# Projecting the last key tiles of two batches together in a cross-attention kernel

## The chip, the cores and the metric

The kernel runs on one core of a Trainium2 chip. Its time is the device time of one execution in microseconds (us), as the median of several runs.

## What is computed

One layer on x (32 batches, 64 tokens, 128 features): cross-attention onto a context of 1601 keys per batch, masked by length, then a windowed self-attention, then a quantized feed-forward part, each added to x. Only the cross-attention is touched:

```
q: layernorm(x) @ Wq, k: ctx @ Wk, v: ctx @ Wv, 16 heads of 64
qh = rms_norm(qh, q_norm_w); kh = rms_norm(kh, k_norm_w)
scores = einsum('bhld,bhsd->bhls', qh, kh) * (1.0 / np.sqrt(HEAD_DIM))
scores = where(s < x_seqlens[b], scores, NEG_INF)
attn = softmax(scores, axis=-1)
x = x + (attn @ vh, heads joined) @ Wo
```

## The kernel before

The context of a batch is cut into NC = 13 key tiles: twelve of P = 128 keys and a last one of LAST = 65. The key weights are folded into the queries beforehand, so the scores come from the raw context. The projection of the keys is still needed for one thing: each key's sum of squares per head, from which the reciprocal of its norm (rrms) is made. A tile of keys, c of batch p (n = p * 13 + c), goes through these steps:

- SyncE loads it in four DMAs into a stage buffer (`load_stage`), in blocks of 32; the last tile has a buffer of its own and a fifth DMA for its last key.
- VectorE turns it (`turn`), ScalarE rounds it to `cT_hi` (`split_hi`), GpSimd forms the rest `cT_lo` (`split_lo`).
- TensorE projects it (`project`): three matmuls into each of two banks, `k_ps0` and `k_ps1`, 512 columns each. ScalarE squares the banks (`square`), VectorE sums them per head into `ssq` (`sum_squares`).
- Ten steps later TensorE computes the scores (`score`, six matmuls into `s_ps0` and `s_ps1`). VectorE masks and scales them into the arena (`scale`) and keeps the maximum over the tiles (`keep_best`).
- Twenty steps after a tile's scores GpSimd subtracts the maximum (`shift`), ScalarE takes the exponential, TensorE multiplies by the context rows (`values`, sixteen matmuls into `u_ps`).

Every engine walks through the same steps (p, c), written by `each_step`, in its own fixed order. In a step (p, c) TensorE does: projection of tile n + 10 (KEYS_AHEAD), scores of tile n, values of tile n - 20. VectorE does: maximum of tile n - 1, scaling of tile n (two halves, with the turn of tile n + 12 between them), sum of squares of tile n + 10. So the last tile of batch p is projected in step 2 of batch p itself. Further work of VectorE per batch: in step 1 it turns the block of maxima (`turn_blocks`, L847), in steps 2 and 3 it reduces it (`best_of_blocks`, L854), in step 2 it forms the mean squares of the late tiles (L809) and in step 3 their norms (`newton`, L69 to L73). GpSimd's shift in a step waits for that step's `keep_best`.

Batches 2 to 30 are a hardware loop of one batch per pass; batches 0, 1, 31 and two draining rounds are written out. Before them come 20 query steps (projection, norm and turning of the queries), into which the first key tiles are woven; `query(i)` is step i. There no values run up to step 7 of batch 1; in these first steps GpSimd folds the squares in half before VectorE sums them (`fold_squares`, L502).

Semaphores are counted by `Turns`: `x.ended(n)` is the count when unit n has been done. The rows of the context that `values` needs are loaded once per batch in step 9 of SyncE.

## Time and profile before

| | |
|---|---|
| median of 3 runs | 2409.81 us (2409.37 to 2410.38) |
| the profiled execution, and its span | 2404.72 us, 2402.9 us |
| TensorE busy | 2310.5 us, 96% |
| VectorE busy | 2094.6 us, 87% |
| GpSimd busy | 1491.6 us, 62% |
| ScalarE busy | 1368.2 us, 57% |
| mean granted TensorE clock | 0.991 |
| query stage, up to the first scores | about 128 us |
| batches 0 and 1 | 128.7 to 231.2 us |
| one batch in the loop | about 59.6 us |

PE is TensorE (PEld its weight loads), DVE VectorE, ACT ScalarE, POOL GpSimd, SP SyncE. A busy time says how long an engine had work in hand; a row of a time line gives the start, the duration and, in square brackets, how long the engine had been idle before and what ended that. Neighbouring matmuls overlap, so start to start is the time one costs.

### The profile page before, as it was taken

The numbers are of one execution on the slowest core, as the hardware profiler recorded it, in microseconds if no ns is written. First come the engines' busy times: TensorE is split into PE (matmuls) and PEld (weight loads), VectorE is DVE, ScalarE is ACT, GpSimd is POOL, SyncE is SP. The second block draws the span as 40 slices with busy tenths as digits, with TensorE's granted clock in tenths as the row PEclk, the third lists the DMA queues.
The fourth block names the chain that finished last, engine by engine and source line by source line (L and its number), as shares of the span: only waits on it lengthen the run. The fifth ranks groups of instructions, "written<-read, shape, count | busy, mean of one in ns | idle before, by whom it ended". The sixth has DMA issues, their size and how long they took to land. (4 is left out here: it accounts for less than half of the span.)

```text
span 2402.9 us, 57401 instructions
## 1 busy us (share of the span) xinstructions
PE 2310.5 (96%) x16343; PEld 1955.8 (81%) x16343; DVE 2094.6 (87%) x3382; ACT 1368.2 (57%) x2594; POOL 1491.6 (62%) x1069
## 2 busy tenths in 40 slices
PE   7988999999999999999999999999999998899985
PEld 4667888888888888888888888888888888788743
DVE  8789999999999999999999999999999998468776
ACT  6744555555555555555555555555555554455646
POOL 4556777777777777777777777777777773001100
PEclk9999999999999999999999999999999999999987
DMA  3431222222222222222222222222222214421000
GB/s 114 182 85 46 55 54 54 54 54 54 54 54 54 54 54 54 54 55 57 57 54 54 54 54 54 54 54 54 54 54 54 54 38 134 155 90 37 2 1 18
DMA packets 442651, 145.04 MB, mean 60 GB/s; under 512 B 365360, under 2 KB 425680, under 8 KB 442448
## 3 DMA queue, kind: packets, MB, share of 16 engines
q1 hardware_dynamic: 442432, 143.50, 24.0%
q8 instruction: 49, 0.80, 0.1%
q10 hardware_dynamic: 144, 0.52, 0.1%
q14 instruction: 26, 0.21, 0.0%
HBM read 109.17 MB, written 34.73 MB: 60 GB/s over the span
## 5 line engine op out<-in xcount | busy, mean ns | idle before, releaser
L465 POOL TENSOR_TENSOR probs<-arena,best_all 128x1024 f32 (+2 forms) x397 | 943.5, 2377 | 420.0 <-DVE best L842 399.3
L1094 PEld LDWEIGHTS u_ps<-rows,probs 128*128 128x128 f32 x6656 | 803.0, 192 | 56.3 <-issue 15.3
L1094 PE MATMUL u_ps<-rows,probs 128*128 (+1 forms) x6656 | 813.9, 276 | 10.0 <-ACT probs L670 5.0
L827 DVE SCALAR_TENSOR_TENSOR arena<-s_ps,mask,rrms 128x512 f32 (+2 forms) x832 | 604.0, 727 | 117.9 <-PE s_ps L971 116.5
L670 ACT ACTIVATE probs<-probs 128x1024 f32<-128x1024 f32 (+1 forms) x416 | 441.5, 1062 | 411.9 <-POOL probs L465 397.5
L802 DVE TENSOR_REDUCE ssq<-squares 128x16 f32<-128x1024 f32 (+2 forms) x416 | 490.7, 1180 | 38.2 <-ACT squares L628 36.6
L628 ACT ACTIVATE squares<-k_ps 128x512 f32<-128x512 f32 (+1 forms) x832 | 452.2, 592 | 42.5 <-PE k_ps L971 22.2
L842 DVE TENSOR_TENSOR best<-best,arena 128x1024 f32<-128x1024 f32 (+1 forms) x352 | 444.7, 1263 | 0.2
L969 PE MATMUL k_ps<-w_hi,cT_hi 128*128 128x512 f32 (+1 forms) x832 | 361.9, 435 | 5.2 <-ACT squares L628 3.5
L622 ACT ACTIVATE cT_hi<-cT 128x128 fp32r<-128x128 f32 (+1 forms) x416 | 130.1, 313 | 367.6 <-DVE cT L793 367.6
L969 PE MATMUL s_ps<-q_hi,cT_hi 128*128 (+2 forms) x832 | 330.4, 397 | 3.3 <-DVE arena L827 3.0
L971 PE MATMUL k_ps<-w_hi,cT_lo 128*128 128x512 f32 (+1 forms) x832 | 328.6, 395 | 0.0
L970 PE MATMUL k_ps<-w_lo,cT_hi 128*128 128x512 f32 (+1 forms) x832 | 327.2, 393 | 0.0
L970 PE MATMUL s_ps<-q_lo,cT_hi 128*128 (+2 forms) x832 | 327.2, 393 | 0.0
L971 PE MATMUL s_ps<-q_hi,cT_lo 128*128 (+2 forms) x832 | 327.1, 393 | 0.0
L507 POOL TENSOR_TENSOR cT_lo<-cT,cT_hi 128x128 fp32r<-128x128 f32 (+1 forms) x416 | 300.3, 722 | 37.1 <-ACT cT_hi L622 36.7
L969 PEld LDWEIGHTS s_ps<-q_hi,cT_hi 128*128 128x128 f32 (+1 forms) x832 | 153.6, 185 | 46.7 <-DVE arena L827 7.4
L971 PEld LDWEIGHTS s_ps<-q_hi,cT_lo 128*128 128x128 f32 (+1 forms) x832 | 153.1, 184 | 40.0
L970 PEld LDWEIGHTS s_ps<-q_lo,cT_hi 128*128 128x128 f32 (+1 forms) x832 | 153.5, 184 | 39.2
L971 PEld LDWEIGHTS k_ps<-w_hi,cT_lo 128*128 128x128 f32 (+1 forms) x832 | 152.9, 184 | 39.5
L969 PEld LDWEIGHTS k_ps<-w_hi,cT_hi 128*128 128x128 f32 (+1 forms) x832 | 154.5, 186 | 33.4 <-issue 8.9
L970 PEld LDWEIGHTS k_ps<-w_lo,cT_hi 128*128 128x128 f32 (+1 forms) x832 | 154.5, 186 | 19.8
(246 smaller groups left out, 2201.4 us busy)
## 6 DMA issues: line engine op xcount, KB each, us to landing
stage<-in_ctx SPq DMA_DIRECT2D x1536, 16.0 KB, 1.7
rows<-in_ctx SPq DMA_DIRECT2D x32, 768.0 KB
queries<-probs SPq DMA_DIRECT2D x16, 1024.0 KB, 4.0
q_plain<-queries SPq DMA_DIRECT2D x32, 512.0 KB, 3.2
best_all<-best_rows SPq DMA_DIRECT2D x31, 512.0 KB, 3.7
u_transposed<-uT_sb SPq DMA_DIRECT2D x124, 128.0 KB, 2.6
a_uT<-u_transposed SPq DMA_DIRECT2D x10, 1024.0 KB, 4.9
arena<-u_transposed SPq DMA_DIRECT2D x6, 1024.0 KB, 5.0
```

What stands on the lines that cost most here:

```text
L465: pool.tensor_tensor(probs[0:r, slot_of(c, PRING), :], scores_at(b, c), best_all[0:r, bass.ds((b % 2) * HL, HL)], ALU.subtract).then_inc(s ...
L507: pool.tensor_tensor(cT_lo[:, c, 0:r], cT[:, 0:r], cT_hi[:, c, 0:r], ALU.subtract).then_inc(lo_ready.sem, 1)
L622: act.activation(cT_hi[:, c, 0:rows_of(c)], cT[:, 0:rows_of(c)], ACT.Copy).then_inc(hi_ready.sem, 1)
L628: act.activation(squares[0:rows_of(c), half(h)], k_ps[h][0:rows_of(c), :], ACT.Square).then_inc(squared.sem, 1)
L670: act.activation(tile, tile, ACT.Exp).then_inc(probs_ready.sem, 1)
L802: dve.tensor_reduce(ssq[0:r, c * H:(c + 1) * H], squares[0:r, :].rearrange("p (h d) -> p h d", d=HD)[:, :, 0:width], AX_X, ALU.add).then_i ...
L827: dve.scalar_tensor_tensor(out=scores_at(p, c, h * HALF, HALF).rearrange("p (h l) -> p h l", l=L), in0=s_ps[h][0:r, :].rearrange("p (h l) ...
L842: dve.tensor_tensor(best[0:r, :], so_far, scores_at(p, c), ALU.max).then_inc(kept.sem, 1)
L969: pe.matmul(out, cT_hi[:, c, 0:r], hi, start=True, stop=False)
L970: pe.matmul(out, cT_hi[:, c, 0:r], lo, start=False, stop=False)
L971: return pe.matmul(out, cT_lo[:, c, 0:r], hi, start=False, stop=True)
L1094: last = pe.matmul(u_ps[g // 3][:, at:at + UW], probs[0:r, s, g * P:(g + 1) * P], rows, start=(c == 0 and g % 3 == 0), stop=(c == NC - 1), ...
```

## The change

Two batches form a pair. The even batch's last tile is filled up: besides its own 65 keys it takes SHARED = 63 keys of the odd batch's last tile (`load_shared`, eight DMAs). It is turned, split, projected, squared and summed with all 128 rows (`key_rows`). The odd batch's last tile is `borrowed`: it is still loaded, turned and split, since its scores need it, but no longer projected, squared, folded or reduced. Its 65 sums of squares come from elsewhere. 63 rows are carried from the even batch's `ssq` to a corner of `tmp` by a DMA (`load_shared_ssq`, step 7 of the even batch); VectorE copies them into place in step 2 of the odd batch. The two keys left over in each pair, 32 in all, form one extra tile, which is loaded, turned, split, projected, squared and reduced within the query steps 3 to 7; its sums go to memory (`left_ssq`), from where each pair's two rows are fetched.

The loop now runs over pairs 1 to 14, with two batches per pass; batch 30 is written out. The load of the context rows moves from SyncE's step 9 to step 11, and one of its waits goes.

```diff
@@ -170,6 +173,13 @@
 QUERY_STEPS = TILES + CARRY_Q
 KEYS_FROM = 5
 CHUNK = 4
+PAIR_KEYS = 2 * NC - 1
+SHARED = P - LAST
+LEFT = LAST - SHARED
+LEFT_KEYS = B // 2 * LEFT
+LEFT_FROM = 3
+LEFT_IN = 16 * LEFT * D // SIDE
+TAIL_IN = (16 * (3 * D // SIDE + 1), 16 * (D // SIDE + 1))
 
 
 def each_step(eng, query, step, keys_from=KEYS_FROM):
@@ -181,14 +191,37 @@
     for p in (0, 1):
         for c in range(NC):
             step(p, c, On(p, c))
-    with eng.Fori(2, B - 1) as p:
-        for c in range(NC):
-            step(p, c, On())
-    for p in (B - 1, B, B + 1):
+    with eng.Fori(1, B // 2 - 1) as pair:
+        for odd in range(2):
+            for c in range(NC):
+                step(pair * 2 + odd, c, On(pair=pair, odd=odd))
+    for p in (B - 2, B - 1, B, B + 1):
         for c in range(NC):
             step(p, c, On(p, c))
 
 
+def tile_ahead(c, on, ahead):
+
+    later, c = divmod(c + ahead, NC)
+    batch = on.odd + later
+    return on.pair + batch // 2, batch % 2, c
+
+
+def key_number(pair, odd, c):
+
+    return pair * PAIR_KEYS + (odd * NC + c)
+
+
+def borrowed(odd, c):
+
+    return odd == 1 and c == NC - 1
+
+
+def key_rows(odd, c):
+
+    return P if odd == 0 else rows_of(c)
+
+
 def slot_of(c, ring):
 
     return c % ring if c < NC - 1 else ring
@@ -251,6 +284,8 @@
         y0 = sb("y0", [P, NC * H])
         tmp = sb("tmp", [P, NC * H])
         rrms = sb("rrms", [P, NC * H])
+        ssq_shared = tmp[:, EARLY * H:EARLY * H + H]
+        ssq_left = ssq_shared[0:LEFT_KEYS, :]
         qkw = sb("qkw", [P, 3])
         len_i = sb("len_i", [P, B], I32)
         cT = sb("cT", [P, P])
...
+            def load_shared(p, s):
+                first = (NC - 1) * P
+                for g in range(D // SIDE):
+                    dims = slice(g * SIDE, (g + 1) * SIDE)
+                    sp.dma_start(stage[g * SIDE + 1:(g + 1) * SIDE, s, 2 * SIDE:3 * SIDE],
+                                 ctx_in[bass.ds(p + 1, 1), first:first + SIDE - 1, dims].rearrange("b k i -> (b k) i")
+                                 ).then_inc(stage_in[s], 16)
+                    sp.dma_start(stage[g * SIDE:(g + 1) * SIDE, s, 3 * SIDE:4 * SIDE],
+                                 ctx_in[bass.ds(p + 1, 1), first + SIDE - 1:first + 2 * SIDE - 1, dims].rearrange("b k i -> (b k) i")
+                                 ).then_inc(stage_in[s], 16)
+
+            def store_left():
+                sp.wait_ge(left_steps, 6)
+                sp.dma_start(left_out, ssq_left[:, :]).then_inc(shared_in, 16)
+
+            def load_shared_ssq(pair, p):
+                sp.wait_ge(rrms_ready.sem, rrms_ready.ended(p, 6))
+                if isinstance(pair, int) and pair == 0:
+                    sp.wait_ge(shared_in, 16)
+                sp.dma_start(ssq_shared[0:SHARED, :], ssq[LAST:P, (NC - 1) * H:NC * H]).then_inc(shared_in, 16)
+                sp.dma_start(ssq_shared[SHARED:LAST, :], left_out[bass.ds(pair * LEFT, LEFT), :]).then_inc(shared_in, 16)
+
+            def load_stage(p, c, odd):
                 s = slot_of(c, RING)
                 sp.wait_ge(turned.sem, turned.ended(p * NC + c - back(c, RING)))
+                if c == NC - 1 and isinstance(p, int) and p == 0:
+                    sp.wait_ge(left_steps, 1)
+                if c == NC - 1 and odd == 0:
+                    load_shared(p, s)
                 if c == 0 and isinstance(p, int) and p == 0:
                     sp.wait_ge(consts_ready, 4)
                 full = rows_of(c) // SIDE
@@ -406,7 +475,13 @@
 
             def step(p, c, on):
                 if on.load:
-                    load_stage(p + 1, c)
+                    load_stage(p + 1, c, 1 - on.odd)
+                if c == 0 and isinstance(p, int) and p == -1:
+                    load_left()
+                if c == NC - 1 and isinstance(p, int) and p == -1:
+                    store_left()
+                if c == 7 and on.scores and on.odd == 0:
+                    load_shared_ssq(on.pair, p)
                 if c == 5 and on.queries:
                     load_q(p + 1)
                 if c == NC - 1 and on.finish and not ending(p):
...
-                if c == 9 and on.scores:
-                    if not isinstance(p, int) or p > 0:
-                        sp.wait_ge(rows_in, p * 32)
-                    sp.wait_ge(valued.sem, valued.ended(p * NC - NC - 1))
+                if c == 11 and on.scores:
+                    sp.wait_ge(valued.sem, valued.ended(p * NC - NC))
...
+                if i == LEFT_FROM + 1:
+                    act.wait_ge(left_steps, 1)
+                    act.activation(cT_hi[:, NC - 1, 0:LEFT_KEYS], cT[:, 0:LEFT_KEYS], ACT.Copy).then_inc(left_steps, 1)
+                if i == LEFT_FROM + 3:
+                    act.wait_ge(left_steps, 4)
+                    for h in range(2):
+                        last = act.activation(squares[0:LEFT_KEYS, half(h)], k_ps[h][0:LEFT_KEYS, :], ACT.Square)
+                    last.then_inc(left_steps, 1)
 
             def split_q_hi(p):
                 act.wait_ge(q_in, p * 16 + 16)
...
-                if on.keys:
+                if on.keys and not borrowed(*tile_ahead(c, on, KEYS_AHEAD)[1:]):
                     for h in range(2):
-                        square(n + KEYS_AHEAD, at_step(p, c, KEYS_AHEAD)[1], h)
+                        square(n + KEYS_AHEAD, *tile_ahead(c, on, KEYS_AHEAD), h)
                 if on.turn:
-                    split_hi(n + TURN_AHEAD, at_step(p, c, TURN_AHEAD)[1])
+                    split_hi(n + TURN_AHEAD, *tile_ahead(c, on, TURN_AHEAD)[1:])
...
+                if i == LEFT_FROM:
+                    dve.wait_ge(stage_in[RING], LEFT_IN)
+                    dve.transpose(cT[:, 0:LEFT_KEYS], stage[:, RING, 0:LEFT_KEYS]).then_inc(left_steps, 1)
+                if i == LEFT_FROM + 4:
+                    dve.wait_ge(left_steps, 5)
+                    dve.tensor_reduce(ssq_left[:, :], squares[0:LEFT_KEYS, :].rearrange("p (h d) -> p h d", d=HD),
+                                      AX_X, ALU.add).then_inc(left_steps, 1)
...
-            def sum_squares(n, c, folded=False):
-                r = rows_of(c)
+            def sum_squares(n, pair, odd, c, folded=False):
+                r = key_rows(odd, c)
+                if borrowed(odd, c):
+                    dve.wait_ge(shared_in, pair * 32 + 48)
+                    dve.tensor_copy(ssq[0:r, c * H:(c + 1) * H], ssq_shared[0:r, :]).then_inc(summed.sem, 1)
+                    return
                 if folded:
-                    dve.wait_ge(halved, n - KEYS_AHEAD + 1)
+                    dve.wait_ge(halved, key_number(pair, odd, c) - KEYS_AHEAD + 1)
                 else:
-                    dve.wait_ge(squared.sem, squared.ended(n))
+                    dve.wait_ge(squared.sem, squared.ended(key_number(pair, odd, c)))
                 width = HD // 2 if folded else HD
                 dve.tensor_reduce(ssq[0:r, c * H:(c + 1) * H],
...
+                if i == LEFT_FROM + 2:
+                    pe.wait_ge(left_steps, 3)
+                    for h in range(2):
+                        last = product(k_ps[h][0:LEFT_KEYS, :], NC - 1, LEFT_KEYS, w_hi[:, half(h)], w_lo[:, half(h)])
+                    last.then_inc(left_steps, 1)
+
+            def project(n, pair, odd, c):
+                r, k = key_rows(odd, c), key_number(pair, odd, c)
                 pe.wait_ge(lo_ready.sem, lo_ready.ended(n))
+                if isinstance(n, int) and n == 0:
+                    pe.wait_ge(left_steps, 5)
                 for h in range(2):
-                    pe.wait_ge(squared.sem, squared.ended(n - 1, h + 1))
-                    product(k_ps[h][0:rows_of(c), :], c, w_hi[:, half(h)], w_lo[:, half(h)]).then_inc(keys.sem, 1)
+                    pe.wait_ge(squared.sem, squared.ended(k - 1, h + 1))
+                    product(k_ps[h][0:r, :], c, r, w_hi[:, half(h)], w_lo[:, half(h)]).then_inc(keys.sem, 1)
 
             def score(p, n, c):
                 if c == 0:
...
-                if on.keys:
-                    project(n + KEYS_AHEAD, at_step(p, c, KEYS_AHEAD)[1])
+                if on.keys and not borrowed(*tile_ahead(c, on, KEYS_AHEAD)[1:]):
+                    project(n + KEYS_AHEAD, *tile_ahead(c, on, KEYS_AHEAD))
```

TensorE, loop, around the projection of the last tile (k_ps: key banks, s_ps: score banks, u_ps: values). Before:

```order
L1094 MATMUL u_ps2<-rows1,probs 128x129 x2
L1038 REGISTER_ALU
L1040 ISA
L969 MATMUL k_ps0<-w_hi,cT_hi 65x512
L970 MATMUL k_ps0<-w_lo,cT_hi 65x512
L971 MATMUL k_ps0<-w_hi,cT_lo 65x512
L1040 REGISTER_ALU
L969 MATMUL k_ps1<-w_hi,cT_hi 65x512
L970 MATMUL k_ps1<-w_lo,cT_hi 65x512
L971 MATMUL k_ps1<-w_hi,cT_lo 65x512
L1051 ISA
L969 MATMUL s_ps0<-q_hi,cT_hi 128x512
```

After, in the odd batch's half of the loop:

```order
L1211 MATMUL u_ps2<-rows1,probs 128x129 x2
L1168 ISA
L1078 MATMUL s_ps0<-q_hi,cT_hi 128x512
L1079 MATMUL s_ps0<-q_lo,cT_hi 128x512
L1080 MATMUL s_ps0<-q_hi,cT_lo 128x512
```

The values of step 1 are now followed at once by the scores of step 2; the six matmuls between them are gone.

VectorE, loop, step 2 (ssq: sums of squares, best_row: reduced maxima, ms: mean squares). Before:

```order
L827 SCALAR_TENSOR_TENSOR arena<-s_ps,mask,rrms 128x512
L800 ISA
L802 TENSOR_REDUCE ssq<-squares 65x16
L854 TENSOR_REDUCE best_row<-u_sb 128x16
L809 TENSOR_SCALAR ms<-ssq 128x80
L840 ISA
L842 TENSOR_TENSOR best<-best,arena 128x1024
```

After, in the odd batch's half:

```order
L938 SCALAR_TENSOR_TENSOR arena<-s_ps,mask,rrms 128x512
L903 ISA
L904 COPY ssq<-tmp 65x16
L965 TENSOR_REDUCE best_row<-u_sb 128x16
L918 TENSOR_SCALAR ms<-ssq 128x80
L951 ISA
L953 TENSOR_TENSOR best<-best,arena 128x1024
```

A copy stands where the reduction stood; all else keeps its place.

## Rows read from the trace of the kernel before

**Rows 1.** Busy time in stretches: us, busy (x instructions), clock, DMA share, GB/s.

```profile
231.00:1960.00 1729.00, 1728.71 (x10587) 1507.22 (x10586) 1587.35 (x2408) 1003.69 (x1886) 1306.03 (x870) 1.00 0.24 54
```

**Rows 2.** Time line of TensorE, batch 19, steps 2 to 5: start, duration, what.

```profile
1252.00 0.48 PE L969 MATMUL k_ps<-w_hi,cT_hi 128*65 128x512 f32 x1
...
1253.46 0.39 PE L969 MATMUL s_ps<-q_hi,cT_hi 128*128 x1
...
1259.43 1.95 PE L1094 MATMUL u_ps<-rows,probs 128*128 x16
...
1268.67 1.96 PE L1094 MATMUL u_ps<-rows,probs 128*128 x16
```

**Rows 3.** Time line of VectorE, batch 19, steps 1, 2 and 6.

```profile
1251.48 1.20 DVE L802 TENSOR_REDUCE ssq<-squares 128x16 f32<-128x1024 f32 x1
...
1253.94 1.23 DVE L842 TENSOR_TENSOR best<-arena 128x1024 f32 x1
...
1256.59 1.20 DVE L802 TENSOR_REDUCE ssq<-squares 65x16 f32<-65x1024 f32 x1
...
1272.90 0.75 DVE L827 SCALAR_TENSOR_TENSOR arena<-s_ps,mask,rrms 128x512 f32 x1 [0.48 <-PE s_ps L971]
```

**Rows 4.** Time line of GpSimd, batch 19, step 2.

```profile
1255.42 2.38 POOL L465 TENSOR_TENSOR probs<-arena,best_all 128x1024 f32 x1 [3.52 <-DVE best L842]
```

**Rows 5.** Time line of ScalarE, batch 19, steps 3 and 5.

```profile
1257.83 1.07 ACT L670 ACTIVATE probs<-probs 128x1024 f32<-128x1024 f32 x1 [1.35 <-POOL probs L465]
1258.80 1.06 ACT L628 ACTIVATE squares<-k_ps 128x512 f32<-128x512 f32 x2
...
1267.38 1.06 ACT L670 ACTIVATE probs<-probs 128x1024 f32<-128x1024 f32 x1 [1.37 <-POOL probs L465]
```

**Rows 6.** Time lines of VectorE and GpSimd in the query stage.

```profile
26.17 1.81 DVE L743 TENSOR_SCALAR arena<-arena 128x16 f32<-128x16 f32 x1
...
30.52 0.18 DVE L743 TENSOR_SCALAR arena<-arena 128x16 f32<-128x16 f32 x1
...
26.05 1.90 POOL L484 TENSOR_TENSOR arena<-arena 128x1024 f32<-128x1024 f32 x1
```

**Rows 7.** Time lines of TensorE and ScalarE, batch 31, steps 2 to 4.

```profile
1970.68 1.95 PE L1094 MATMUL u_ps<-rows,probs 128*128 128x129 f32 x16
1972.38 0.48 PE L969 MATMUL s_ps<-q_hi,cT_hi 128*128 128x512 f32 x1
...
1974.33 2.05 PE L1094 MATMUL u_ps<-rows,probs 128*128 128x129 f32 x16 [0.31 <-ACT probs L670]
1976.14 0.48 PE L969 MATMUL s_ps<-q_hi,cT_hi 128*128 128x512 f32 x1
...
1973.22 1.06 ACT L670 ACTIVATE probs<-probs 128x1024 f32<-128x1024 f32 x1 [3.14 <-POOL probs L465]
```

**Rows 8.** Time lines of VectorE and GpSimd, batch 1, step 2.

```profile
181.21 2.30 DVE L842 TENSOR_TENSOR best<-arena 128x1024 f32<-128x1024 f32 x1
...
184.95 0.66 DVE L802 TENSOR_REDUCE ssq<-squares 65x16 f32<-65x512 f32 x1
...
181.15 1.28 POOL L502 TENSOR_TENSOR squares<-squares 65x512 f32<-65x512 f32 x1 [1.49 <-ACT squares L628]
```

**Rows 9.** Time lines of TensorE and ScalarE, query step 6 and its end.

```profile
40.49 0.66 PE L1000 MATMUL u_ps<-ident,arena 128*128 128x128 f32 x4 [0.58 <-ACT probs L582]
...
46.84 0.31 ACT L622 ACTIVATE cT_hi<-cT 128x128 fp32r<-128x128 f32 x1 [0.22 <-DVE cT L793]
```

**Rows 10.** DMA queues, 231 to 291 us, then 400 to 1900: packets, MB, share.

```profile
q8 instruction: 3, 0.05, 0.4%
...
q1 hardware_dynamic: 337891, 80.98, 24.3%
```

**Rows 11.** The loop's branch line at 1240 to 1243 us, and the weight loads behind.

```profile
L184 PEldq COMPARE_BRANCH x1: 208/208/208, 1240.8 to 1240.8; - x1
...
1242.84 0.19 PEld L969 LDWEIGHTS k_ps<-w_hi,cT_hi 128*128 128x128 f32 x1
```

97 lines of the change are left out of this document (61 added, 36 removed).

## Prediction

> **What bounds the kernel now.** I read the busy times of the long middle stretch first, then the time line of one odd batch on every engine, then the places where the pattern breaks (batch 1, batch 31, the query stage).
>
> From 231 to 1960 us runs the loop over batches 2 to 30. TensorE is busy 1728.7 of its 1729 us, VectorE 1587 (92%), GpSimd 1306, ScalarE 1004, and the granted clock is 1.00, the upper level of 2.4 GHz [rows 1]. A step (one key tile) takes about 4.57 us on TensorE: projection 1.46, scores 1.4, values 1.7. So at first sight every matmul taken out shortens the time. But "busy" only says that TensorE's gaps are small, not that the other engines have room. The question is how early each tile's exponentials are ready before TensorE wants them.
>
> Take batch 19, an odd one inside the loop. Step 2 holds the projection that the change removes. It starts at 1252.00 and the scores after it at 1253.46: 1.46 us, with 65 keys in the tile [rows 2]. One step later, in step 3, TensorE starts the values matmuls at 1259.43 [rows 2]. Their exponentials ended at 1257.83 + 1.07 = 1258.90 [rows 5]: only 0.53 us in hand. In step 5 it is worse: values at 1268.67 [rows 2], exponentials ended 1267.38 + 1.06 = 1268.44 [rows 5], 0.23 us in hand. That is no accident of one tile. VectorE carries extra work in steps 1 to 4 (turning the best-score block, two reductions of it, the late key norms) and falls behind: it has no idle time until step 6, where it waits 0.48 us for scores again [rows 3].
>
> How little can be in hand? Batch 31 shows it, since from its step 3 on the kernel projects no keys, and its TensorE step is as short as the changed one. There the exponentials end at 1973.22 + 1.06 = 1974.28 and the values start at 1974.33, marked as waiting for ScalarE [rows 7]: 0.05 us is the least. The step shows a second price: values to next scores takes 1976.14 - 1974.33 = 1.81 us after a wait, against 1972.38 - 1970.68 = 1.70 without one [rows 7]. A wait costs 0.11 us to refill the pipe.
>
> **The odd batches in the loop (14 of them).** Removed are six matmuls of 1.46 us in step 2. The chain that ends in step 3's exponentials doesn't use them: VectorE's best-score maximum at 1253.94, GpSimd's subtraction 1255.42 to 1257.80 [rows 3, 4], ScalarE's exponential to 1258.90 [rows 5]. Nor can that chain start sooner, since VectorE's run-up to it begins with the scores of step 1, ahead of the removed work. So step 3's values move from 1259.43 to 1258.90 + 0.05 = 1258.95: 0.48 us gained, 0.98 lost to the new wait. After the refill 0.37 us is left for what follows.
>
> Then step 5. Its room is 0.23 - 0.05 = 0.18 us, unless VectorE gets faster as well. VectorE loses the reduction at 1256.59, 1.20 us long, and gets a copy of 65x16 in its place [rows 3]. The copy is small, but where it stands counts: it would start at about 1256.59, in the middle of GpSimd's subtraction (until 1257.80). The query stage has just such a pair. VectorE's L743, 128x16, takes 0.18 us with GpSimd's long operation not running, and 1.81 us where that one starts just before it: it ends at 27.98, GpSimd's operation at 26.05 + 1.90 = 27.95 [rows 6]. So I take it that the copy is held until GpSimd is done and ends at 1257.83, against 1257.79 for the reduction. VectorE is not earlier but 0.04 us later. Step 5's values then move by 0.18 - 0.04 = 0.14 us, less another refill of 0.11: 0.03 us per odd batch, **0.4 us for 14**. From step 6 on VectorE waits for TensorE again, and the small gain stays.
>
> The Trainium skill ("SBUF — State Buffer", section "SBUF: two separate sides") states this as a rule: one port pair is shared by VectorE and GpSimd under an exclusive lock, and the loser is blocked for the other's whole instruction; the trace agrees. Without this rule the copy would take some 0.2 us and the next rival would be the forecast.
>
> Even batches: the last tile has 128 keys in place of 65. The matmuls write 512 columns per row either way, and the reduction takes 1.20 us for 128 rows and for 65 [rows 3]. I cost this at nothing; should a row count matter after all, it falls in step 2 of even batches, where nothing is taken out and step 3 still has its 0.53 us in hand.
>
> **Batch 1.** No values run before step 7, so VectorE leads. Its maximum takes 2.30 us instead of 1.2, since GpSimd's folding of the very tile that is now borrowed starts 0.06 us before it [rows 8]. The fold goes (1.1 us), and the reduction of 0.66 becomes a copy of about 0.2, with no GpSimd work to hold it: 0.4. Together **-1.5 us** (bounds 0 and -2.5: the projection, the fold and the reduction gone, against other work that fills in).
>
> **Batch 31.** Its step 3 is bound by the same chain today, and the copy meets GpSimd's subtraction again. **0** (bounds 0 and -1.0).
>
> **The extra tile of 32 keys** runs in the query stage: on TensorE 1.46 us at the end of its step 5, of which the 0.58 us idle in the next step absorbs a part [rows 9]: 0.9. Two squares on ScalarE, 1.06 us [rows 5], where it idles only 0.22 us: 0.8. A transpose and a reduction (0.3 and 1.13) on VectorE and two small splits (0.3 and 0.46): VectorE is partly idle there, and GpSimd waits: 0.8. Together **+2.5 us**; bounds 0 (all of it in gaps) and 4.7 (their plain sum).
>
> **SyncE.** Eight more DMAs for each even batch's last tile, two for the sums of squares, and the load of the rows moved from step 9 to step 11. All are read or used a full three steps (13 us) or more after they are issued, and the last tile's issue is followed by a wait for the transposed result. Cost 0; if the cover failed, it would show as VectorE waiting for a stage DMA.
>
> **Sum.** -0.4 - 1.5 + 0 + 2.5 = +0.6 us: 2404.7 us of the profiled execution becomes 2405.3. The median of the runs is 5.1 us above that execution (2409.8), so I forecast **2410.4 us**. A difference under 0.2% (4.8 us) can't be told from no change.
>
> **Rival 1: the copy isn't held.** [Rows 6] show a one-input arithmetic operation, not a copy. If it runs through, VectorE is up to 1.0 us earlier from step 3 on, step 5 isn't tight any more, and the 0.37 us of step 3 survives: 14 x 0.37 = 5.2, batch 31 gains 1.0, and with -1.5 + 2.5 the sum is -5.2 us: 2404.6. For it: the operation differs. Against it: same engine, same kind of operands, same width. Chance 0.18.
>
> **Rival 2: TensorE's saving counts in full**, as its 99.98% busy share suggests: 16 x 1.46 = 23.4, less 2.5: 2388.9 us. It needs step 3's exponentials 1 us earlier than today; nothing ahead of them changes. Chance 0.05.
>
> **Rival 3, slower: the loop's code no longer stays on the engines.** The loop's body now holds two batches. In its first pass, 231 to 291 us, TensorE's instruction queue brought in three packets [rows 10], each 0.4% x 16 x 60 / 3 = 1.3 us long; from 400 to 1900 us only the data queue moved anything [rows 10]. So the old body stays resident; a doubled one may not, and then each of 13 jumps back waits for code. TensorE's branch is at 1240.8 and the first weights of the next pass load at 1242.84 [rows 11]: 2.0 us of waiting are hidden. A delay of one packet costs nothing; two packets and a DMA's way of 1.4 us (the shortest landing in the profile's list of DMAs) would be 4.0 us by estimate, 2.0 of them seen: 13 x 2.0 = 26 us, 2436. It decides from a delay of 2.4 us a pass. Chance 0.10.
>
> The Trainium skill ("Runtime: NRT & Kernel Launch", section "Instruction fetch mechanics") says that a taken branch whose target isn't in the current two-page window forces a DMA fetch, which speaks against a doubled body; the trace of the old loop differs, since it brought three pages in and none again. By the rule alone the old loop would have fetched as well, and the change would halve the number of fetches.
>
> **How the numbers follow.** Forecast 0.62 (2408 to 2412, mostly by the extra tile), rival 1 0.18, rival 2 0.05, rival 3 0.10, and 0.05 for the extra tile at its full price with batch 1 giving nothing. The range 2402 to 2415 takes in the forecast, rival 1 and the bounds of the extra tile. Faster by over 0.2%, 0.21: rival 2, half of rival 1 (it lies on the limit), some of the forecast's lower end. Slower, 0.15: rival 3 and the extra tile's upper end. Within, 0.64.
>
> **What the changed profile would show.** In an odd batch, values of step 3 marked as waiting for the exponentials, about 0.9 us, and in step 5 again; the copy at L904 lasting over 1 us and ending together with GpSimd's subtraction; a step of 3.1 us followed by one near 5.5; 119 us for a pair of batches, as before. Rival 1: a copy of 0.2 us. Rival 3: packets of the instruction queues between 400 and 1900 us. Wrong I'd be if the pair took under 118.5 us or over 120.

## The result

The changed kernel takes **2430.01 us** in the median of 6 runs (2423.69 to 2435.53), the kernel before 2407.82 in 6 runs beside it (2402.83 to 2410.38). The ratio is 1.0095, with a 95% interval of 1.0075 to 1.0115: about 0.95% **slower**. The forecast was 2410.4 us with a range of 2402 to 2415, so it was wrong. The profiled execution of the changed kernel took 2423.69 us, the fastest of its six.

Its page, head and queues (columns as before):

```profile
span 2421.9 us, 55706 instructions
...
PE 2297.6 (95%) x16253; PEld 1947.5 (80%) x16253; DVE 2118.3 (87%) x3384; ACT 1345.0 (56%) x2565; POOL 1378.3 (57%) x1069
...
q14 instruction: 229, 1.88, 0.3%
q8 instruction: 55, 0.90, 0.2%
```

The saving is there in the busy times: TensorE 13 us and ScalarE 23 us less than in the table of before. GpSimd's 113 us less is another matter: it runs 1069 operations as before, but its splits `cT_lo` of 128 keys take 0.47 us in the mean from 400 to 1900 us, where they took 0.77. The kernel e1 below, which shares nothing, shows the same (1381 us busy), so this isn't the sharing's. The span is 19.0 us longer all the same. Two more views say where to look. The first is the same stretch of time as [rows 1], the second the DMA queues of the changed kernel from 400 to 1900 us, where before only the data queue q1 appeared [rows 10]:

```profile
231.00:1960.00 1729.00, 1697.94 (x10375) 1483.15 (x10374) 1590.88 (x2377) 973.57 (x1838) 1181.52 (x860) 1.00 0.25 54
```

```profile
q1 hardware_dynamic: 336368, 80.03, 24.3%
q14 instruction: 184, 1.51, 0.4%
```

To see which steps grew I took the start of every tile's first score matmul and subtracted neighbours; the length of step k is here the time from its scores to those of step k + 1. From the two profiled executions, in us:

```
                                  before    changed   difference
first scores (query stage)         128.7      130.9       +2.2
batches 0 and 1                    102.57     100.54      -2.0
loop, 14 even batches, mean         59.62      61.51      +1.89 each, +26.5
loop, 14 odd batches, mean          59.62      59.20      -0.42 each,  -5.9
batch 30                            59.52      59.51       0
batch 31 (to its last scores)       45.72      45.78      +0.1
behind                             397.0      395.2       -1.8
```

The whole loss sits in the even batches of the loop, and there in a single step: step 0 takes 6.69 us in the mean over batches 4 to 28 (4.58 before), 8.41 at the first of them and 6.35 to 6.74 at the others. Those are the 13 steps that follow a jump back. At the first one TensorE's matmuls also run slowly: behind a wait of 1.96 us the granted clock is 0.62 in the mean from 353.7 to 358.2 us (part of it at the lower level of 1.2 GHz), and it is 1.00 in the same step of the 12 other batches. So about 1.9 us of the loss is the clock's, and a jump by itself costs 2.0. Here is the jump at 470 us, first the loop's branch line on each engine (engine, operation, count, duration in ns, first and last start):

```profile
L194 PEldq COMPARE_BRANCH  x1: 220/220/220, 469.2 to 469.2; - x1
L194 PEldq FUSED_REGOPS  x1: 59/59/59, 469.5 to 469.5; - x1
...
L194 DVEq COMPARE_BRANCH  x1: 63/63/63, 470.0 to 470.0; - x1
L194 POOLq FUSED_REGOPS  x1: 59/59/59, 470.2 to 470.2; - x1
...
L194 ACTq COMPARE_BRANCH  x1: 45/45/45, 471.1 to 471.1; - x1
L194 DVEq FUSED_REGOPS  x1: 98/98/98, 473.6 to 473.6; - x1
L194 SPq FUSED_REGOPS  x1: 74/74/74, 474.4 to 474.4; - x1
L194 ACTq FUSED_REGOPS  x1: 59/59/59, 474.9 to 474.9; - x1
```

FUSED_REGOPS is the first instruction of the next pass. TensorE and GpSimd reach it 0.3 us after their branch. VectorE needs 3.6 us, SyncE 3.3, ScalarE 3.8. Then the time lines of GpSimd, ScalarE and TensorE at the same place:

```profile
469.89 2.38 POOL L538 TENSOR_TENSOR probs<-arena,best_all 128x1024 f32<-128x1024 f32 x1 [2.42 <-DVE best L953]
...
475.00 1.06 ACT L763 ACTIVATE probs<-probs 128x1024 f32<-128x1024 f32 x1 [3.68 <-issue]
...
476.11 0.71 PE L1211 MATMUL u_ps<-rows,probs 128*128 128x129 f32 x4 [1.83 <-ACT probs L763]
```

GpSimd's shift is done at 472.27, but ScalarE has no code to take the exponential with until 474.9 ("issue" means that it waited for nothing the profile shows). TensorE waits 1.83 us for it.

### The profile page after: what moved, and what is told of

Read it like the earlier page. It is cut to its first block and busy times, and to the rows that moved or that the text cites. A ratio compares the mean times of both kernels' runs of the same rounds, so it can differ in the third digit from the quotient of the medians.

```text
span 2421.9 us, 55706 instructions
## 1 busy us (share of the span) xinstructions
PE 2297.6 (95%) x16253; PEld 1947.5 (80%) x16253; DVE 2118.3 (87%) x3384; ACT 1345.0 (56%) x2565; POOL 1378.3 (57%) x1069
## 5 line engine op out<-in xcount | busy, mean ns | idle before, releaser
L538 POOL TENSOR_TENSOR probs<-arena,best_all 128x1024 f32<-128x1024 f32 (+1 forms) x397 | 943.7, 2377 | 541.1 <-DVE best L953 513.8
L1211 PE MATMUL u_ps<-rows,probs 128*128 128x129 f32 x6656 | 813.9, 276 | 41.9 <-ACT probs L763 37.0
L938 DVE SCALAR_TENSOR_TENSOR arena<-s_ps,mask,rrms 128x512 f32<-128x512 f32 (+1 forms) x832 | 603.3, 726 | 96.0 <-PE s_ps L1080 84.8
L911 DVE TENSOR_REDUCE ssq<-squares 128x16 f32<-128x1024 f32 (+1 forms) x400 | 471.8, 1179 | 34.1 <-ACT squares L722 32.8
L953 DVE TENSOR_TENSOR best<-best,arena 128x1024 f32<-128x1024 f32 (+1 forms) x352 | 469.8, 1335 | 19.2 <-issue 19.1
L722 ACT ACTIVATE squares<-k_ps 128x512 f32<-128x512 f32 x800 | 433.5, 591 | 30.0 <-PE k_ps L1080 13.3
L1078 PE MATMUL s_ps<-q_hi,cT_hi 128*128 128x512 f32 (+1 forms) x832 | 332.3, 399 | 3.8 <-DVE arena L938 3.7
L1079 PE MATMUL s_ps<-q_lo,cT_hi 128*128 128x512 f32 (+1 forms) x832 | 327.4, 393 | 0.0
L1080 PE MATMUL s_ps<-q_hi,cT_lo 128*128 128x512 f32 (+1 forms) x832 | 327.3, 393 | 0.0
L587 POOL TENSOR_TENSOR cT_lo<-cT,cT_hi 128x128 fp32r<-128x128 f32 (+1 forms) x416 | 195.1, 469 | 47.1 <-ACT cT_hi L713 46.8
```

Of the source, the lines that this page charges most:

```text
L538: pool.tensor_tensor(probs[0:r, slot_of(c, PRING), :], scores_at(b, c), best_all[0:r, bass.ds((b % 2) * HL, HL)], ALU.subtract).then_inc(s ...
L587: pool.tensor_tensor(cT_lo[:, c, 0:r], cT[:, 0:r], cT_hi[:, c, 0:r], ALU.subtract).then_inc(lo_ready.sem, 1)
L722: act.activation(squares[0:r, half(h)], k_ps[h][0:r, :], ACT.Square).then_inc(squared.sem, 1)
L911: dve.tensor_reduce(ssq[0:r, c * H:(c + 1) * H], squares[0:r, :].rearrange("p (h d) -> p h d", d=HD)[:, :, 0:width], AX_X, ALU.add).then_i ...
L938: dve.scalar_tensor_tensor(out=scores_at(p, c, h * HALF, HALF).rearrange("p (h l) -> p h l", l=L), in0=s_ps[h][0:r, :].rearrange("p (h l) ...
L953: dve.tensor_tensor(best[0:r, :], so_far, scores_at(p, c), ALU.max).then_inc(kept.sem, 1)
```

## The experiments

Two theories. **Code**: the doubled loop body no longer stays on some engines and is fetched again at each jump back. **Transfers**: the longer step comes from something else that the change does around the same place (ten more DMAs per pair, the moved load of rows, the waits on SyncE's queue).

### The loop doubled without the change, and the change without loops

e1 takes the kernel before and only doubles the loops of four engines:

```
+        with eng.Fori(1, B // 2 - 1) as pair:
+            for odd in range(2):
+                for c in range(NC):
+                    step(pair * 2 + odd, c, On())
```

> The kernel before, nothing shared: only the loops of TensorE, VectorE, ScalarE and GpSimd take two batches per pass (batch 30 written out), SyncE's stays at one. Code theory (VectorE's and ScalarE's loop bodies of 408 and 286 instructions no longer stay at hand, each of the 13 jumps back costs 2.0 us, the first 3.9 as in the changed kernel): 13 x 2.0 + 1.9 = 28 us on top of before, about 2433. Transfer theory (the longer first step of the even batches comes from the shared tile's extra loads and waits on SyncE's queue): nothing of that is here, so no difference from before, within 2 us.

Measured 2409.27 us, ratio 1.0020 (1.0011 to 1.0029); VectorE's and ScalarE's bodies are 381 and 285 instructions in the trace. The direction is that of the code theory, not the size: 5 us, not 28. The jumps are there, 122 packets of the instruction queue between 400 and 1900 us, and ScalarE is held 2.5 to 3.0 us at each. But step 0 grows from 4.58 to 5.25 us only.

e2 takes the changed kernel and writes out VectorE's, ScalarE's and SyncE's steps:

```
+    if straight:
+        for p in range(2, B - 2):
+            for c in range(NC):
+                step(p, c, On(p, c))
```

> The changed kernel with the code of VectorE, ScalarE and SyncE written out without a loop; TensorE and GpSimd keep theirs over two batches. Code theory: no jump back on the three engines, the first steps of the even batches fall from 6.5 to 4.6 us, 28 us less than the changed kernel, 2396 to 2403 against 2405 to 2408 of before, if odd batches keep their 59.2 us. Transfer theory: the extra transfers are all still there, so the first steps stay at 6.5 us and the time at that of the changed kernel, 0.9% above before.

2395.89 us, 0.9972 (0.9961 to 0.9983). Step 0 is back at 4.58 us, with every transfer of the change still there. So the transfers by themselves cost nothing there, and the loss needs the code to be fetched. What e2 doesn't exclude is that the transfers lengthen a fetch: ScalarE's jump takes 2.8 us in the mean in e1 and 2.5 in e18, which share nothing, but 3.2 in e3 and 3.7 in the changed kernel. e2 shows too what the change is worth without the fetches, 0.28% faster. e8 makes sure that this isn't owed to writing out as such:

> The kernel before with VectorE, ScalarE and SyncE written out, nothing shared. Its jumps back of 0.2 to 0.3 us are off TensorE's path, so the code theory expects no difference from before, within 0.1%: the straight changed kernel owes its gain to the sharing. If written-out code were itself faster, it would show here, up to 29 x 0.1 = 3 us; if its running fetches disturb, slower.

2404.07 us, 0.9983 (0.9973 to 0.9992): a little under before, by about what writing out was allowed to bring. In its profile the gain is in the stall that before has in step 7 of the batches (a mean of 4.63 us there instead of 4.69; 4.56 in the straight changed kernel). So of the 0.28% of e2 a part may belong to the written-out code; 0.1% lies between the two ratios, and their intervals overlap.

### Which engine pays

> The changed kernel with VectorE and SyncE written out; of the three engines only ScalarE still jumps back over 279 instructions. If ScalarE's late exponential is what TensorE waits for: first steps of even batches near 6.0 to 6.5 us, 20 to 26 us more than with all three written out. If VectorE's late maximum alone did it: first steps at 4.6 us, as with all three written out.

> The changed kernel with ScalarE and SyncE written out; of the three engines only VectorE still jumps back, over 383 instructions. If VectorE's delay of 3.6 us (keep_best, then GpSimd's shift, then the scaling) is on TensorE's path: first steps near 6 us, 15 to 26 us more than with all three written out. If only ScalarE's delay counts: first steps at 4.6 us, no more than with all three written out.

e3: 2416.39 us, 1.0053 (1.0039 to 1.0068), step 0 at 6.05 us. e4: 2404.10 us, 0.9995 (0.9985 to 1.0005), step 0 at 4.58 and step 1 at 4.9 us. ScalarE's time line and TensorE's at the jump of e3:

```profile
472.24 1.06 ACT L768 ACTIVATE probs<-probs 128x1024 f32<-128x1024 f32 x1 [3.14 <-issue]
...
473.35 0.82 PE L1216 MATMUL u_ps<-rows,probs 128*128 128x129 f32 x5 [1.24 <-ACT probs L768]
```

So ScalarE's fetch is the dear one, 1.47 us seen per jump; VectorE's, though as long (3.8 us), costs 0.3, since it has done its part for the exponential of step 0 before it jumps. With all three fetching it is 2.1. What SyncE's adds was measured on the fastest kernel (below): nothing by itself.

> The straight kernel with the early turn, except that SyncE keeps its loop of 437 instructions and its jump of 3.1 us. SyncE issues loads many steps ahead of their use: if so, no difference from the straight one, 0.9884 of before (0.987 to 0.990), step lengths all alike. If SyncE's jump counted, up to 13 x 0.5 = 6 us more.

2380.24 us, 0.9899 (0.9883 to 0.9915), against 0.9884 (0.9868 to 0.9900) without SyncE's loop, and all step lengths are alike, although its jump takes 2.9 us.

### How long a body may be

In the trace one pass counts 206 instructions on VectorE before, 145 on ScalarE, 208 on SyncE, 91 on GpSimd. Changed it is 387, 280, 437 and 142 (GpSimd stays). I padded the old loops with increments of a semaphore that nobody reads, at each step's end:

```
             step(p, c, On())
+            for _ in range(pad):
+                eng.sem_inc(padded, 1)
```

> The kernel before, its loop of one batch per pass, with semaphore increments that nobody waits for added to each step's end: 7 on ScalarE (145 instructions a pass become 236), 3 on VectorE (206 become 245), 2 on SyncE (208 become 234), 12 on GpSimd (91 become 247). If a body of up to 256 instructions (two packets of 8 KB) stays, no engine shows a delay at the jump back and the queue of instructions is empty from 400 to 1900 us. If the limit lies nearer to 206, the engines over it show a delay of 2.5 to 3.8 us at each jump. By way of the pads alone: VectorE and ScalarE 0.1 to 0.3 us later per step, which may cost TensorE some 0.1 us a step.

> As the one before with more: ScalarE 262 instructions a pass, VectorE 258, SyncE 273, GpSimd 273. If the limit is 256, all four show a delay of 2.5 to 3.8 us at each jump back, the first of them GpSimd, whose loop of 142 had none. If the limit is about 276 (280 missed, 273 not), none does.

Neither has a late engine or a packet of an instruction queue from 400 to 1900 us. The longest of e11, SyncE's and GpSimd's 273 instructions and ScalarE's 262, stay. (Their 2411.41 and 2417.26 us, one run each, come from elsewhere: by the pads step 5 takes 4.8 to 4.9 us instead of 4.6, and e11's first scores, ahead of all pads, are 5 us later than before.) My limit of 256 was wrong. But 280 on ScalarE do not stay. Either the limit lies between 273 and 280, or something else than length decides.

The packets give a hint. Between 400 and 1900 us the straight kernel runs 7216 instructions on the three engines (by the trace) and brings in 57 packets (its row of the queue view follows): 127 instructions in each, so I take 128 to a packet of 8 KB.

```profile
q14 instruction: 57, 0.47, 0.1%
```

```
             act.wait_ge(qkw_ready, 1)
+            for _ in range(32):
+                act.sem_inc(qkw_ready, 1)
```

The trace then has 457 instructions ahead of the loop, 31 more: one increment takes the place of a separate wait.

> The changed kernel with 32 semaphore increments on ScalarE at its very beginning, where it waits anyway: its loop starts 32 instructions later, its length stays 280. 
> The kernel before, one batch per pass, with ScalarE's body padded from 145 to 353 instructions (16 increments in each step) and the same 32 ahead. Place theory: it begins 9 to 26 instructions into a packet and ends within the third, so no delay at the jump, although it is 73 longer than the one that missed. Length theory: a delay of 2.5 to 3.8 us at each jump.

e13: **2400.31 us, 0.9985 (0.9976 to 0.9995)**. Thirty-two idle instructions at the start of one engine's program take 1.1% off the changed kernel. Branch and first instruction of the next pass, ScalarE, VectorE and SyncE:

```profile
L194 DVEq COMPARE_BRANCH  x1: 63/63/63, 468.3 to 468.3; - x1
...
L194 ACTq COMPARE_BRANCH  x1: 45/45/45, 469.2 to 469.2; - x1
L194 ACTq FUSED_REGOPS  x1: 59/59/59, 469.4 to 469.4; - x1
L194 SPq COMPARE_BRANCH  x1: 54/54/54, 469.4 to 469.4; - x1
L194 DVEq FUSED_REGOPS  x1: 98/98/98, 471.9 to 471.9; - x1
L194 SPq FUSED_REGOPS  x1: 74/74/74, 472.4 to 472.4; - x1
```

ScalarE goes on after 0.2 us, its exponential waits for GpSimd again, and the queue of the same stretch has 60 packets less, 5 for each of 12 jumps:

```profile
q14 instruction: 124, 1.02, 0.2%
```

e14, the body of 353 from the moved place, in the same two views (branch line, then queues):

```profile
L184 ACTq COMPARE_BRANCH  x1: 45/45/45, 471.2 to 471.2; - x1
L184 ACTq FUSED_REGOPS  x1: 50/50/50, 471.4 to 471.4; - x1
```

```profile
q1 hardware_dynamic: 335988, 80.74, 24.2%
```

No delay and no packet, with 73 instructions more than the body that missed; its one run took 2404.21 us, beside 2404.46 of before. So length alone is refuted, and the place counts.

The size of the blocks was still open: 128 instructions, of which a body may touch three, or 256, of which it may touch two. Both fit everything up to here. Two more kernels tell them apart, the edits as above with 129 in place of 32, and with 20 pads in each step in place of 16.

> The changed kernel with ScalarE's loop of 280 instructions moved by 128 (129 increments, of which one takes the place of a wait), not by 32. Blocks of 128: the loop begins at the same place within a block as in the changed kernel, so the delay of 3.7 us is there at each jump and the time is that of the changed kernel, about 2430. Blocks of 256: the loop begins 105 to 122 instructions into a block and touches two, so no delay at ScalarE's jump and about 2400 us, as when it is moved by 32.

> The kernel before, ScalarE's body padded to 405 instructions (20 increments in each step), begun at the place where 353 stayed. Blocks of 128: it touches four blocks, so a delay of 2.5 to 3.8 us at each of 28 jumps and some five packets for each, 120 of them from 400 to 1900 us. Blocks of 256: it begins 9 to 26 instructions into a block and ends within the second, so no delay and no packet.

e17 took 2431.79 us (before 2408.84 beside it), ScalarE is held 3.4 to 4.0 us at each jump, and there are 184 packets again, as in the changed kernel to the packet. (The time alone would prove little: with 129 increments at the start the first scores come at 142.1 us instead of 130.9.) e18 took 2460.48 us, its step 0 in every batch of the loop 1.9 us longer. ScalarE's branch line at a jump, and the queue from 400 to 1900 us:

```profile
L184 ACTq COMPARE_BRANCH  x1: 45/45/45, 476.1 to 476.1; - x1
L184 ACTq FUSED_REGOPS  x1: 50/50/50, 478.5 to 478.5; - x1
```

```profile
q14 instruction: 123, 1.01, 0.2%
```

123 packets over 25 jumps are 4.9 a jump; four touched and one ahead had been worked out as 120. Moved by 31, the loop of 280 stays; moved by 128, it is fetched as at first; 353 fit and 405 don't. The reading with blocks of 128 and three of them safe fits every kernel here, and the one with 256 is refuted. (e14, e17 and e18 ran once each, but their jumps agree with each other, 13 or 28 of them in a trace.) It stays a reading: where the blocks begin was inferred from what stayed, and only on ScalarE was a loop moved.

### The saving that didn't come through

In an odd batch step 1 takes 3.10 us instead of 4.55, since step 2's projection is gone. Of this 0.9 us is lost in step 3 (5.46; the expectations below call it step 4, after the scores that end it) and 0.2 in step 5. Time lines of TensorE, ScalarE, VectorE and GpSimd, changed kernel, batch 7, steps 2 and 3:

```profile
541.97 0.48 PE L1078 MATMUL s_ps<-q_hi,cT_hi 128*128 128x512 f32 x1
...
548.81 2.05 PE L1211 MATMUL u_ps<-rows,probs 128*128 128x129 f32 x16 [0.62 <-ACT probs L763]
...
547.70 1.06 ACT L763 ACTIVATE probs<-probs 128x1024 f32<-128x1024 f32 x1 [1.29 <-POOL probs L538]
...
542.53 1.24 DVE L958 STREAM_TRANSPOSE u_sb<-best 128x1024 f32<-128x1024 f32 x1
543.87 1.23 DVE L953 TENSOR_TENSOR best<-arena 128x1024 f32<-128x1024 f32 x1
...
546.53 1.16 DVE L904 COPY ssq<-tmp 65x16 f32<-65x16 f32 x1
...
545.25 2.41 POOL L538 TENSOR_TENSOR probs<-arena,best_all 128x1024 f32<-128x1024 f32 x1 [3.43 <-DVE best L953]
```

Read backwards from 548.81: exponential, shift, maximum (L953), and ahead of that `turn_blocks` (L958), 1.24 us. That turn needs only the maxima of the batch before, so it can stand at the start of step 1, where VectorE waits for scores:

```
+                if on.rows and c == 1 and not draining(p):
+                    turn_blocks(p - 1)
                 if on.scores:
                     scale(p, n, c, 0)
```

> The changed kernel with VectorE, ScalarE and SyncE written out, and turn_blocks moved from the end of VectorE's step 1 to its start, ahead of the scaling. Chain theory (the odd batch's spared projection of 1.46 us comes back because the exponentials of steps 3 to 5 wait for shift, keep_best and, in front of them, turn_blocks): keep_best of step 2 starts 1.2 us earlier, step 4 of an odd batch falls from 5.43 towards 4.6, the odd batch gains 0.6 to 1.2 us, 16 x 0.6 to 1.2 = 10 to 19 us under the straight kernel without it, 2377 to 2386. Capacity theory (VectorE is simply full in steps 2 to 5 of an odd batch, its reduction having turned into a copy held by GpSimd's shift): the odd batch stays at 59.2 us and the time within 3 us of 2396.

**2379.91 us, 0.9884 (0.9868 to 0.9900)**. All odd batches take 58.10 us, against 59.41 with the same early turn and no sharing (e6 below): 1.3 of the 1.46 us come through. The same places in batch 19 of this kernel:

```profile
1239.37 0.48 PE L1083 MATMUL s_ps<-q_hi,cT_hi 128*128 128x512 f32 x1
...
1245.42 1.83 PE L1216 MATMUL u_ps<-rows,probs 128*128 128x129 f32 x15
...
1243.71 1.06 ACT L768 ACTIVATE probs<-probs 128x1024 f32<-128x1024 f32 x1 [1.35 <-POOL probs L543]
...
1235.32 1.24 DVE L963 STREAM_TRANSPOSE u_sb<-best 128x1024 f32<-128x1024 f32 x1
1237.27 0.75 DVE L943 SCALAR_TENSOR_TENSOR arena<-s_ps,mask,rrms 128x512 f32<-128x512 f32 x1 [0.72 <-PE s_ps L1085]
...
1242.57 1.14 DVE L909 COPY ssq<-tmp 65x16 f32<-65x16 f32 x1
...
1241.29 2.38 POOL L543 TENSOR_TENSOR probs<-arena,best_all 128x1024 f32<-128x1024 f32 x1 [2.17 <-DVE best L958]
```

From step 2's scores to step 3's exponentials it was 5.73 us and is 4.34. The values wait for nobody. The turn runs in idle time (0.72 us of it are left behind it), and the copy is still held until GpSimd is done (1.14 us, until 1243.71), without harm. The control on the kernel before:

> The kernel before with turn_blocks moved in the same way, nothing else. TensorE sets the step there, with 0.04 us of stall a batch, so both theories expect no more than 1 us: within 0.1% of before. A gain here would mean that the turn was on the path without any sharing.

2398.23 us, 0.9962 (0.9949 to 0.9975). I had expected nothing. Its profile shows 3.9 us less in batches 0 and 1 (batch 1's step 2 takes 3.29 us instead of 5.30; 1.7 us of the 3.9 are a difference in the clock, see the end) and 4.5 us in the loop, where the stall of step 7 is gone (4.55 us instead of 4.69). So of e5's 1.2% about 0.4% could be had without sharing.

The copy was the other suspect (rival 1). e9 gives it to ScalarE:

```
+                elif on.keys:
+                    act.wait_ge(shared_in, on.pair * 32 + 48)
+                    act.wait_ge(summed.sem, summed.ended(n + KEYS_AHEAD - 1))
+                    act.activation(ssq[0:LAST, (NC - 1) * H:NC * H], ssq_shared[0:LAST, :], ACT.Copy).then_inc(summed.sem, 1)
```

> The changed kernel with VectorE, ScalarE and SyncE written out, and the odd batch's copy of the borrowed sums made by ScalarE in place of VectorE, so that GpSimd's shift can't hold it there. Lock theory (rival 1 of the prediction, the copy of 1.15 us keeps VectorE late for steps 3 to 6): VectorE is 0.9 us earlier from step 3 on, step 5 of an odd batch falls from 4.81 to 4.6 and step 4 towards 5.2, an odd batch 0.23 to 0.6 us shorter, 14 x = 3 to 8 us, 2388 to 2393 against 2395.9. Turn theory (the exponentials of step 3 hang on turn_blocks and keep_best ahead of the copy, step 4 inherits it): at most the 0.23 us of step 5, and values of step 3 still wait 0.6 us.

2393.60 us, 0.9955 (0.9938 to 0.9972). ScalarE copies in a fifth of the time, and TensorE waits in step 3 as before:

```profile
538.70 0.22 ACT L777 ACTIVATE ssq<-tmp 65x16 f32<-65x16 f32 x1 [0.56 <-DVE ssq L918]
...
544.80 1.38 PE L1218 MATMUL u_ps<-rows,probs 128*128 128x129 f32 x10 [0.61 <-ACT probs L768]
```

Step 5 falls from 4.80 to 4.57 us, the odd batch from 59.21 to 58.94: the turn theory's figure. Batch 31 gains 0.7 us besides. But the kernel isn't quite the case of a copy that nothing holds, since with the copy gone GpSimd's subtraction holds VectorE's next small operation. VectorE and GpSimd at that place:

```profile
543.11 0.60 DVE L925 TENSOR_SCALAR ms<-ssq 128x80 f32<-128x80 f32 x1
543.64 1.52 DVE L960 TENSOR_TENSOR best<-best,arena 128x1024 f32<-128x1024 f32 x1
...
541.25 2.41 POOL L543 TENSOR_TENSOR probs<-arena,best_all 128x1024 f32<-128x1024 f32 x1 [3.52 <-DVE best L960]
```

The mean squares take 0.60 us instead of 0.18 and end close to GpSimd's operation. Counted from step 2's scores, the next maximum ends only 0.4 us earlier than in the changed kernel, not the 1.0 us that rival 1 had for VectorE.

### The extra tile

e7 leaves out the extra tile of 32 keys, so the norms of two keys of each pair aren't computed:

> The straight kernel without the extra tile of 32 keys in the query steps (its sums are a constant, so the norms of two keys per pair are left out of the computation). By the prediction's term the tile costs 2.5 us: 2393.4 against 2395.9. If the query stage has room for it: no difference. If it disturbs the stage further than its own matmuls: up to 5 us.

2396.73 us, 0.9955 (0.9942 to 0.9968) of its own before, against 0.9972 with the tile. The intervals overlap: by the times the tile costs 4 us, give or take 4. The profiles say more once the granted clock is looked at. First scores come at 128.7 to 134.8 us in all kernels but e17, with or without the tile, but the late ones are mostly profiles whose clock fell on the way there: 0.955 in the mean from 20 us on in e4, with 134.8 us, and 1.00 in before and in the changed kernel. Where it was 1.00 all that way, batch 1's first scores come at 172.2, 173.0 and 172.9 us without the tile (before, e8, e18) and at 175.5, 175.6 and 175.1 with it (changed, e3, e5): 2.7 us apart. e7 and e2, both at 0.98, are 1.9 us apart. So by these profiles the tile costs 2 to 3 us, as predicted, and batch 0 pays a part of it.

### Both repairs with the loops kept

> The changed kernel as it is, with its loops over two batches on every engine, and only turn_blocks moved to the start of VectorE's step 1. If the two effects add up: odd batches 58.1 us as in the straight kernel with the same move, batch 31 1.3 us shorter, so 16 to 18 us less than the changed kernel, 2412 to 2414 and still above before by 0.2 to 0.4%. If the early turn also lets ScalarE reach its jump back sooner, more than that. If the jumps swallow the gain: about 2428.

> The changed kernel, all loops kept, with ScalarE's 32 increments ahead and the turn at the start of VectorE's step 1. Place theory: the two add up, odd batches 58.1, even ones 59.9 us; 13 x 1.75 = 23 us less than with the turn alone, ratio to before 0.992 to 0.994, about 2387. Length theory: as with the turn alone, 1.002.

e12: 2409.05 us, 1.0021 (1.0012 to 1.0031), odd batches at 58.09 us, step 0 still at 6.67. e16: **2383.35 us, 0.9910 (0.9896 to 0.9924)**. The two add up, and with loops of two batches on every engine this is 1.8% under the changed kernel by the two ratios, and 0.3% above the straight one, partly by VectorE's fetch (step 1 at 4.74 us instead of 4.55, 13 times).

## Why the prediction was wrong

**The step that failed is the doubled loop body: the sum gave it nothing, and rival 3, which priced it, looked at the wrong engine and had a chance of 0.10.** Measured, the even batches of the loop lost 26.5 us in the profile, 1.9 of them by the clock. The prediction's sign for rival 3 came, packets of an instruction queue in the middle of the loop, and so did its sign of being wrong, a pair of batches over 120 us (120.7). That rival 3's price was almost exact (2.0 us a jump; measured 2.11, or 2.0 without the clock's part; 2436 us against 2430) is luck. It took 4.0 us of delay less 2.0 hidden on TensorE; measured were 3.7 us of delay on ScalarE, with 1.6 hidden in the wait for GpSimd's shift and in what ScalarE has in hand. "A doubled one may not [stay], and then each of 13 jumps back waits for code" was followed on TensorE alone, where 2.0 us of waiting are hidden. TensorE's body of 1617 instructions in a pass stays. The engines with small bodies were never counted: ScalarE's 280, VectorE's 387 and SyncE's 437 are what is fetched again, and ScalarE has only about 0.8 us in hand at that place when nothing is fetched. Straight kernel, the same step, ScalarE and TensorE:

```profile
468.22 1.06 ACT L768 ACTIVATE probs<-probs 128x1024 f32<-128x1024 f32 x1 [1.35 <-POOL probs L543]
...
470.09 1.72 PE L1216 MATMUL u_ps<-rows,probs 128*128 128x129 f32 x14
```

The exponential ends at 469.28, and the values start at 470.09. [Rows 10] could only say that the old bodies fit. A loop body on every engine should have been counted against the packets, and a chance of 0.10 was far too low for something that nothing in the trace bounded.
The other steps, in the order of the prediction:

- **Odd batches, -0.4 us for 14.** The mechanism was right: values of step 3 wait for the exponentials (0.62 us), step 5 gives a little back, the copy lasts 1.16 us and ends at 547.69, GpSimd's shift at 547.66. The size was low. Against e1, which has the same loop without sharing (59.42), the straight kernel's odd batches take 59.21, 0.2 us less each, not 0.03. And all batches lost the stall that before has in step 7 (4.69 us against 4.56), 3.6 us in 28 batches, which the sum hadn't. That isn't the sharing's: e1, which shares nothing, lost it too (4.56 us). What removed it stays open. Without the fetches the kernel is 6.7 us under before by e2's ratio, where the sum said +0.6.
- **"Nor can that chain start sooner"** was wrong as a statement on the kernel, though right for the change as made. `turn_blocks` stood in the chain and had no need to (e5). For the same reason rival 2's 1.46 us a batch was a real price: 1.3 came through once the turn was moved.
- **Rival 1** needed the copy free of GpSimd. Giving it to ScalarE was worth 0.27 us an odd batch (e9), 3.8 us for 14 against its 5.2, and 0.7 for batch 31 against its 1.0.
- **Even batches, 0 for the fuller tile:** held; 59.51 us in the straight kernel, 59.62 before.
- **Batch 1, -1.5:** batches 0 and 1 together gave -2.0, which agrees in part by luck. The mechanism is there: the maximum of step 2 takes 1.22 us instead of 2.30, and steps 1 to 4 of batch 1 took 15.5 us instead of 16.9. But batch 0 took 1.0 us more, and step 7 of batch 1 took 1.7 less because of the clock (see the end). **Batch 31, 0:** +0.1. **SyncE, 0:** held, even with its own jump of 3 us (e15).
- **Extra tile, +2.5:** 2 to 3 us by the profiles with like clocks.

## What to carry to other kernels

When a change lengthens a hardware loop, count the instructions of one pass on every engine, also on those that are half idle. Here the one that hurt most was ScalarE, with little in hand right behind its jump, and neither TensorE, whose body is the longest, nor VectorE and SyncE, whose bodies are longer and were fetched as well. The sign is packets of an instruction queue in the middle of the loop and a late first instruction behind the branch, with "issue" as the reason; a few idle instructions ahead of the loop can then be worth more than the optimisation. And where a busy engine is relieved and nothing comes of it, read its next wait backwards: work that stands in the chain without belonging there (`turn_blocks`, 1.24 us) was the whole difference between 0.2 and 1.3 us a batch.

## What the runs showed of the hardware

A loop of 280 instructions on ScalarE was fetched at each jump back in one place, not at all 31 instructions later, and again 128 instructions later.
- Such a jump takes 2.4 to 4.2 us. On ScalarE it was 3.2 us when it fetched alone in e3 and 3.7 with VectorE and SyncE fetching too, but 2.5 alone in e18 and 2.8 together with VectorE in e1, whose 5 us in place of 28 come in part from this. What sets it is open.
- A wait at a jump can be followed by a slower TensorE. Step 0 of batch 4 in the changed kernel took 8.41 us and that of batch 18 in e12 8.38, each with a granted clock of 0.80 over the step; at 1.00 the others took 6.3 to 6.8. TensorE had waited 1.96 and 1.95 us before, but waits of 1.96 and 1.98 us at two other jumps of e12 left the clock at 1.00, so the wait's length alone doesn't tell.
- Step 7 of batch 1, where TensorE waits 2.2 us for the first values, takes 7.0 us in the nine profiles where the clock stays at 1.00 and 8.6 to 8.7 in the eleven where it is 0.80. This can swallow a gain made ahead of it: the early turn shortened step 2 of that batch from 5.56 to 3.24 us in e5, and with step 7 at 8.6 us batches 0 and 1 together took 100.8 us against 100.5; in e12, with the same turn and step 7 at 7.0, they took 99.2.
- VectorE's copy of 65x16 took 1.15 to 1.17 us in the 14 odd batches of the changed kernel's loop, ending with GpSimd's long operation, and 0.36 us in batch 1 beside a short one; ScalarE's copy of the same took 0.22 us. Not every operation is held: the reduction that the copy replaced took its 1.20 us in the middle of the same GpSimd operation [rows 3, 4].
